# Softplus attention: softplus as one activation function, its square divided among three engines, experts picked by rank, loops written out

## The chip, the cores and the metric

The kernel runs on one core of a Trainium2 chip. A core has five engines that work through queues of their own and meet at semaphores: TensorE (PE in the profile, its weight loads PEld), VectorE (DVE), ScalarE (ACT), GpSimd (POOL) and SyncE (SP, which issues DMA transfers here). The metric is the device time of one execution in microseconds, lower is better.

## The reference, cut to what matters

The program is a chain of six stages on `x` of shape (4, 1024, 256): a gated recurrent feed-forward, an attention, the feed-forward again, a mixture of experts, a state-space layer, the mixture again. The change touches the attention's inner function and the choice of experts:

```
scores = einsum('bhqd,bhkd->bhqk', q, k) * hs ** (-0.5)      # 16 heads of 16, t = 1024
p = softplus(scores);  p = p * p;  p = p * causal
attn = p / (sum(p, -1) + 1e-09)
out = einsum('bhqk,bhkd->bhqd', attn, v)

gates = softmax(x @ gate_w.T + gate_b)                       # 8 experts
top_gates, top_idx = top_k(gates, 2)
expert_out = einsum('bsh,eoh->bseo', x, expert_w) + expert_b
result = (take(expert_out, top_idx) * top_gates).sum(2)
```

## The kernel before

The stages follow one another, each in a `Phase` that ends with a barrier of all engines: load, feed-forward (`ffn_phase`), queries, keys and values (`qkv_phase`), attention (`attention_phase`), projection, feed-forward, mixture (`moe_phase`), state space (`ssm_phase`), mixture. Each engine's program is written by hand; the order in it is the order of the code, and counted semaphores join the engines. Most stages write their first and last round out and put the rounds between into a hardware loop (`Fori`), in which places and counts come from registers.

**Attention.** Four heads are one pass over 1024 queries; 16 passes make the stage, two to a body, so eight bodies, of which the first and the last are written out and six come from a loop. A pass is cut into 18 units (`pass_units`), a body into `NU` = 36. The queries come in two blocks of 512. Units 0 to 3 are the first block's tiles on the causal diagonal ("rest" units: two pieces per head, each with a small matmul with `neg` that masks it), unit 4 holds its upper pieces in one half-wide bank; units 5 to 12 are the second block's full tiles of 512 columns, 13 to 16 its rest units, 17 its upper unit. So a pass has 8 full, 8 rest and 2 upper units; the first two kinds are 128x1024 numbers, an upper one 128x512.

A unit passes through these hands:

- PE, `score_unit` (L1346, mask L1349, upper unit's mask L1338): scores into one of three pairs of PSUM banks (`SU` = 3).
- ACT, `exp` (L1408): exp of the scores into the weights tile `Wt` in SBUF, which holds `WU` = 12 units; then `ln` (L1414): ln(1 + that), in place. Together they are softplus.
- DVE, `softplus` (L1445): the larger of that and the score itself, which guards large scores; it reads the scores' bank a last time, in two instructions, and so frees it for PE (`max_done`).
- POOL (L1508): the square, in place (`sq_pool`).
- PE, `value_unit` (L1369): the squares times the values and a column of ones, in fp32, into one of two output banks, one for each query block.

PE's program puts the scores of unit u + 7 (`AHEAD`) ahead of the value products of unit u. A block that is complete is copied out by DVE (L1452, 7 units after the block's end), turned by PE (`turn_output`, L1378, 4 units after it), and on DVE the row sums are inverted (L1458, L1460, 9 units after) and the output divided (L1467, 10 units after), which sets `o_done`. PE waits for `o_done` before the first value products of the same query block in the next pass. For the second query block, whose last unit is 17, that is unit 23, while its turn stands behind the value products of unit 21. POOL also copies the values of a pass into `v_ones` (L1499, L1501).

**Mixture.** 16 groups of 512 rows in each of two stages run on PE in matmuls of 512 columns (L48); DVE adds each expert's result, scaled by its gate, to `X` (L932), from a ring of four PSUM banks. In the middle of a group's last tile DVE chooses the experts of the next group (`choose`): softmax, the eight largest by `max` (L899), their places (L902), the first two places compared with a row of numbers `iota` (L908), both added (L912), times half the gates (L914), then a split for PE (L917, L919).

## Time and profile before

| what | us |
|---|---|
| median of 3 runs (1795.97 to 1798.01) | 1797.84 |
| the profiled execution, span from first to last instruction | 1794.8 |
| PE busy in the span | 1683.5 (94%) |
| DVE busy | 1295.7 (72%) |
| ACT busy | 1092.9 (61%) |
| POOL busy | 858.2 (48%) |
| attention, PE's first to last instruction | 274.5 to 815.1 |

The profiled execution's own span is 3.0 us below the median of the runs, which also hold what lies around the span. The profile is read by stage, since each stage is limited by something else. Matmuls are pipelined and the ends of their records are modelled, so a PE that counts as busy may still be waiting; the distance between the starts of two matmuls tells more than a record's length.

### The profile page before, as it was taken

How to read it: one execution, taken by the hardware profiler on the slowest of the kernel's cores; microseconds unless marked ns; L12 is line 12 of the kernel's file. 1: busy time of each engine (PE TensorE's matmuls, PEld its weight loads, DVE VectorE, ACT ScalarE, POOL GpSimd, SP SyncE). 2: the span in 40 equal slices, each digit the busy share in tenths (PEclk: the TensorE clock that was granted, in tenths of full speed). 3: DMA queues.
4: the chain of work that ended last, by engine and by line, in shares of the span. 5: the costliest groups of instructions: out<-in, count | busy, mean ns of one | idle time of the engine just before them, and what ended most of it. 6: DMA issues, size and time to landing. Idle time of an engine off the chain costs nothing. (4 is left out here: it accounts for less than half of the span.)

```text
span 1794.8 us, 33269 instructions
## 1 busy us (share of the span) xinstructions
PE 1683.5 (94%) x11188; PEld 1158.1 (65%) x11188; DVE 1295.7 (72%) x2830; ACT 1092.9 (61%) x1612; POOL 858.2 (48%) x654
## 2 busy tenths in 40 slices
PE   8999897999999999998999899998899999889999
PEld 7888773333333333338788777777677777667777
DVE  5455885777777777775545788886787787778886
ACT  3332788999999999993333322214888887722120
POOL 0002108999999999995003322211265665411111
PEclk9999998999999999999999999999999999999999
DMA  5000275635535535400000100001232233200000
GB/s 164 1 0 12 91 214 90 76 48 73 68 47 73 67 47 79 62 1 1 13 1 30 29 7 0 0 0 39 83 96 95 104 112 103 95 1 24 23 23 24
DMA packets 57112, 95.09 MB, mean 53 GB/s; under 512 B 7904, under 2 KB 29632, under 8 KB 57024
## 3 DMA queue, kind: packets, MB, share of 16 engines
q1 hardware_dynamic: 56064, 93.35, 24.0%
q8 instruction: 51, 0.84, 0.2%
q10 hardware_dynamic: 960, 0.59, 0.1%
q14 instruction: 37, 0.30, 0.1%
HBM read 76.88 MB, written 17.04 MB: 52 GB/s over the span
## 5 line engine op out<-in xcount | busy, mean ns | idle before, releaser
L1508 POOL TENSOR_TENSOR att_weights<-att_weights 128x1024 f32<-128x1024 f32 (+1 forms) x288 | 508.9, 1799 | 9.0 <-DVE att_weights L1445 5.6
L1445 DVE SCALAR_TENSOR_TENSOR att_weights<-att_weights,ps 128x512 f32<-128x512 f32 x544 | 348.2, 684 | 145.1 <-ACT att_weights L1414 138.6
L932 DVE SCALAR_TENSOR_TENSOR X<-ps,moe_gsel,X 128x256 f32 (+1 forms) x512 | 246.6, 484 | 63.1 <-PE ps L48 44.8
L1369 PE MATMUL ps<-att_weights,att_v_ones 64*32 64x64 f32 (+5 forms) x2048 | 289.0, 399 | 1.9 <-POOL att_weights L1508 1.8
L1414 ACT ACTIVATE att_weights<-att_weights 128x1024 f32<-128x1024 f32 (+1 forms) x288 | 286.5, 1007 | 1.0
L1408 ACT ACTIVATE att_weights<-ps 128x1024 f32<-128x1024 f32 (+1 forms) x288 | 278.4, 972 | 8.6 <-PE ps L1349 7.0
L48 PE MATMUL ps<-w_experts_hi,moe_xh 128*128 128x512 f32 x512 | 205.3, 401 | 0.4 <-DVE X L932 0.4
L48 PE MATMUL ps<-w_experts_hi,moe_xl 128*128 128x512 f32 x512 | 203.2, 397 | 0.0
L48 PE MATMUL ps<-w_experts_lo,moe_xh 128*128 128x512 f32 x512 | 201.6, 394 | 0.0
L1369 PEld LDWEIGHTS ps<-att_weights,att_v_ones 128*32 128x32 f32 (+1 forms) x2048 | 82.4, 108 | 104.6 <-issue 80.2
L424 ACT ACTIVATE ffn_gates<-ps,ffn_gate_bias 128x512 f32<-128x512 f32 x72 | 49.5, 688 | 147.5 <-PE ps L48 143.2
L998 POOL TENSOR_TENSOR X<-X,moe_bias_sb 128x512 f32 (+1 forms) x32 | 41.3, 1290 | 193.6 <-DVE X L932 170.8
L1346 PE MATMUL ps<-q_stack,k_stack 128*64 128x64 bf16 (+5 forms) x640 | 103.8, 274 | 23.3 <-DVE att_weights L1445 14.9
L104 POOL TENSOR_TENSOR ffn_rstd<-ffn_var,ffn_power 128x4 f32<-128x4 f32 x14 | 14.1, 1008 | 219.6 <-DVE ffn_var L136 219.6
L1346 PE MATMUL ps<-att_q_stack,att_k_stack 128*64 128x64 bf16 (+5 forms) x640 | 100.5, 267 | 17.0 <-DVE att_weights L1445 13.0
L48 PEld LDWEIGHTS ps<-w_experts_hi,moe_xh 128*128 128x128 f32 x512 | 96.1, 188 | 27.5 <-DVE X L932 4.0
L2172 POOL TENSOR_TENSOR ssm_rise<-ssm_rise,ssm_cT 128x512 f32<-128x512 f32 x56 | 87.8, 1588 | 48.4 <-DVE ssm_xc L2035 37.0
L48 PEld LDWEIGHTS ps<-w_experts_lo,moe_xh 128*128 128x128 f32 x512 | 96.1, 188 | 22.3
L1346 PEld LDWEIGHTS ps<-q_stack,k_stack 128*128 128x128 bf16 (+1 forms) x640 | 42.0, 105 | 104.7 <-DVE att_weights L1445 74.9
L48 PEld LDWEIGHTS ps<-w_experts_hi,moe_xl 128*128 128x128 f32 x512 | 96.2, 188 | 20.4
L1346 PEld LDWEIGHTS ps<-att_q_stack,att_k_stack 128*128 128x128 bf16 (+1 forms) x640 | 40.8, 103 | 98.1 <-DVE att_weights L1445 72.2
L833 ACT ACTIVATE moe_gT<-ps 96x512 fp32r<-96x512 f32 x16 | 9.5, 595 | 155.1 <-PE ps L764 155.1
(282 smaller groups left out, 3796.3 us busy)
## 6 DMA issues: line engine op xcount, KB each, us to landing
ssm_lb<-decays SPq DMA_DIRECT2D x32, 512.0 KB, 4.7
ssm_rise<-decays SPq DMA_DIRECT2D x28, 512.0 KB, 3.9
qk_parts<-qkv_part SPq DMA_DIRECT2D x32, 384.0 KB, 2.7
q_stack<-qk_parts SPq DMA_DIRECT2D x64, 128.0 KB, 4.9
k_stack<-qk_parts SPq DMA_DIRECT2D x64, 128.0 KB, 8.4
att_q_stack<-qk_parts SPq DMA_DIRECT2D x64, 128.0 KB, 4.7
att_k_stack<-qk_parts SPq DMA_DIRECT2D x64, 128.0 KB, 8.5
out<-X SPq DMA_DIRECT2D x7, 512.0 KB, 2.9
```

The costliest lines, as they stand in the source:

```text
L48: ins = pe.matmul(out, l(k), r(k), start=first and n == 0, stop=last and n == len(passes) - 1)
L104: pool.tensor_tensor(self.rstd[:, s], self.var[:, s], self.power[:, :], ALU.pow).then_inc(self.rstd_done, 1)
L424: act.activation(gates[:, m, gate], ring[:, u % RING], ACT.Tanh if gate == 2 else ACT.Sigmoid, bias=bias[:, gate * KC + m:gate * KC + m + ...
L932: dve.scalar_tensor_tensor(out=x, in0=ring[:, e // 2, (e % 2) * C:(e % 2 + 1) * C], scalar=gsel[:, s, j, e:e + 1], in1=x, op0=ALU.mult, op ...
L998: pool.tensor_tensor(x, x, bias_sb[:, turn], ALU.add).then_inc(added, 1)
L1346: ins = pe.matmul(scores(u)[rows, t, c:c + w], SK[s][:, h, keys], SQ[s][:, h, q:q + w], start=not upper, stop=n >= len(segments) - 2 if up ...
L1369: ins = pe.matmul(O(qb)[h * 2 * HD:(h + 1) * 2 * HD, q0:q0 + w], values, Wt[rows, u % WU, t, c:c + w], start=kj == 0 and part == FULL, sto ...
L1408: act.activation(Wt[:, u % WU, 0:n], scores(u)[:, 0:n], ACT.Exp).then_inc(exp_done, 1)
L1414: act.activation(wt, wt, ACT.Ln, bias=1.0).then_inc(ln_done, 1)
L1445: dve.scalar_tensor_tensor(out=wt[:, t], in0=wt[:, t], scalar=LIMIT, in1=scores(u)[:, t], op0=ALU.min, op1=ALU.max).then_inc(max_done, 2 // n)
L1508: pool.tensor_tensor(wt, wt, wt, ALU.mult).then_inc(sq_pool, 1)
L2172: ins = pool.tensor_tensor(heads, heads, cT[:, v, b].unsqueeze(1).broadcast_to([P, NH // 2, P]), ALU.mult)
```

## The change

1. Attention: ACT applies `Softplus` once, straight from the scores' bank (L1405 of the changed kernel), in place of exp and ln; DVE's step with the maximum is gone. `p_done`, set by ACT, frees the bank for PE, in one wait per unit where there were two. The square is divided: of the 18 units of a pass ACT squares units 8 and 14 (L1410), POOL unit 11 (L1495), DVE the other 15 (L1432), 13 of them 128x1024 and two 128x512. PE waits for the engine that squared the unit.
2. Mixture: instead of maxima and places, DVE compares all pairs of the 8 gates (128x256 numbers for four tiles), equal and greater; equal counts only against an earlier expert (`earlier`, a table of 8x8), the two are added and summed to a rank, and gates of rank under 2 are kept.
3. Every `Fori` becomes a Python loop, so all rounds are written out with constant places and counts.

```diff
@@ -895,23 +894,20 @@
                                   ALU.mult).then_inc(prob_done, 1)
                 dve.wait_ge(prob_done, n + 1)
                 dve.tensor_scalar(half[:, :, :], prob[:, :, :], 0.5, None, ALU.mult)
-                for j in range(GT):
-                    dve.max(best[:, j], prob[:, j])
-                dve.drain()
-                for j in range(GT):
-                    ins = dve.max_index(place[:, j], best[:, j], prob[:, j])
-                ins.then_inc(place_done, 1)
-                dve.wait_ge(place_done, n + 1)
-                dve.tensor_copy(placef[:, :, :], place[:, :, 0:2]).then_inc(placef_done, 1)
-                dve.wait_ge(placef_done, n + 1)
-                for r in range(2):
-                    ins = dve.tensor_tensor(pick[:, r], iota[:, :].unsqueeze(1).broadcast_to([P, GT, E]),
-                                            placef[:, :, r:r + 1].broadcast_to([P, GT, E]), ALU.is_equal)
-                ins.then_inc(pick_done, 1)
-                dve.wait_ge(pick_done, n + 1)
-                dve.tensor_tensor(pick[:, 0], pick[:, 0], pick[:, 1], ALU.add).then_inc(both_done, 1)
-                dve.wait_ge(both_done, n + 1)
-                dve.tensor_tensor(gsel[:, s], half[:, :, :], pick[:, 0], ALU.mult).then_inc(gsel_done, 1)
+                others = prob[:, :, :].unsqueeze(2).broadcast_to([P, GT, E, E])
+                own = prob[:, :, :].unsqueeze(3).broadcast_to([P, GT, E, E])
+                dve.tensor_tensor(level[:, :, :, :], others, own, ALU.is_equal).then_inc(level_done, 1)
+                dve.tensor_tensor(above[:, :, :, :], others, own, ALU.is_gt)
+                dve.wait_ge(level_done, n + 1)
+                dve.tensor_tensor(level[:, :, :, :], level[:, :, :, :], earlier[:, :, :].unsqueeze(1).broadcast_to([P, GT, E, E]),
+                                  ALU.mult).then_inc(earlier_done, 1)
+                dve.wait_ge(earlier_done, n + 1)
+                dve.tensor_tensor(above[:, :, :, :], above[:, :, :, :], level[:, :, :, :], ALU.add).then_inc(above_done, 1)
+                dve.wait_ge(above_done, n + 1)
+                dve.tensor_reduce(rank[:, :, :], above[:, :, :, :], AX.X, ALU.add).then_inc(rank_done, 1)
+                dve.wait_ge(rank_done, n + 1)
+                dve.scalar_tensor_tensor(out=gsel[:, s], in0=rank[:, :, :], scalar=2.0, in1=half[:, :, :],
+                                         op0=ALU.is_lt, op1=ALU.mult).then_inc(gsel_done, 1)
                 dve.wait_ge(gsel_done, n + 1)
                 dve.wait_ge(gT_turned, n)
                 dve.tensor_copy(g3[:, :, 0:TERMS:2, 0:E], gsel[:, s].unsqueeze(2).broadcast_to([P, GT, 2, E])).then_inc(g3_hi, 1)
...
@@ -1285,7 +1281,12 @@
     TURN_LAG, COPY_LAG, DEN_LAG, OUT_LAG = 4, 7, 9, 10
     SU, WU = 3, 12
     assert NU % SU == 0 and NU % WU == 0
-    LIMIT = 60.0
+    BY_ACT, BY_POOL = (8, 14), (11,)
+    squarer = ["act" if u % PU in BY_ACT else "pool" if u % PU in BY_POOL else "dve" for u in range(NU)]
+
+    def squares(by, i, u):
+
+        return i * squarer.count(by) + squarer[:u + 1].count(by)
 
     def outputs_at(x, ends, n, lag, i, first, stage):
 
...
@@ -1328,19 +1329,15 @@
                 s, segments = u // PU, pass_units[u % PU]
                 if u % PU == 0:
                     pe.wait_ge(loaded[s], (i + 1) * (16 * 2 * COPIES))
-                half = -1
                 upper = segments[0][-1] == UPPER
+                pe.wait_ge(p_done, i * NU + u + 1)
                 if upper:
                     low = slice(0, HALF)
-                    pe.wait_ge(max_done, 2 * (i * NU + u) + 1)
                     pe.sem_inc(scores_free, 1)
                     for r in range(2):
                         pe.matmul(scores(u)[r * HALF:(r + 1) * HALF, 0].rearrange("p (s q) -> p s q", q=HALF), neg[low, low],
                                   ident16[low, low].unsqueeze(1).broadcast_to([HALF, BANK // HALF, HALF]), start=True, stop=False)
                 for n, (h, kj, t, c, q, w, part) in enumerate(segments):
-                    if t != half and not upper:
-                        half = t
-                        pe.wait_ge(max_done, 2 * (i * NU + u) + t + 1)
                     rows = slice(h % 2 * HALF, (h % 2 + 1) * HALF) if part == UPPER else slice(0, P)
                     keys = slice(kj * P, kj * P + (HALF if part == UPPER else P))
                     ins = pe.matmul(scores(u)[rows, t, c:c + w], SK[s][:, h, keys], SQ[s][:, h, q:q + w],
@@ -1358,7 +1355,7 @@
                     pe.wait_ge(o_done, (i * 2 + s) * BLOCKS + qb + 1)
                     if qb == 0:
                         pe.matmul(O(qb), ident16[:, :], neg[:, 0:1].broadcast_to([P, BANK]), start=True, stop=False)
-                pe.wait_ge(sq_pool, i * NU + u + 1)
+                pe.wait_ge(sq_done[squarer[u]], squares(squarer[u], i, u))
                 if products[0][-1] == UPPER:
                     pe.sem_inc(squared, 1)
                 for h, kj, unit, t, c, q, w, part in products:
@@ -1390,60 +1387,49 @@
             for u in range(AHEAD):
                 score_unit(0, u)
             body(0, first=True)
-            with pe.Fori(1, BODIES - 1) as i:
+            for i in range(1, BODIES - 1):
                 body(i)
             body(BODIES - 1, last=True)
 
         @block.scalar
         def _(act):
-            act.preload_act_table_set(LN_EXP_SET)
-
-            def exp(i, u):
+            act.preload_act_table_set(SOFTPLUS_SET)
+
+            def softplus(i, u):
                 i, u = i + u // NU, u % NU
                 act.wait_ge(s_done, i * NU + u + 1)
 
                 before = step_of[u - WU] + NS if u >= WU else step_of[u - WU + NU]
                 act.wait_ge(pv_done, i * NS + before + 1)
                 n = BANKS[u % PU]
-                act.activation(Wt[:, u % WU, 0:n], scores(u)[:, 0:n], ACT.Exp).then_inc(exp_done, 1)
-
-            def ln(i, u):
-                i, u = i + u // NU, u % NU
-                act.wait_ge(exp_done, i * NU + u + 1)
+                act.activation(Wt[:, u % WU, 0:n], scores(u)[:, 0:n], ACT.Softplus).then_inc(p_done, 1)
+
+            def square(i, u):
+                act.wait_ge(p_done, SU + i * NU + u + 1)
                 wt = Wt[:, u % WU, 0:BANKS[u % PU]]
-                act.activation(wt, wt, ACT.Ln, bias=1.0).then_inc(ln_done, 1)
-
-            def body(i, first=False, last=False):
+                act.activation(wt, wt, ACT.Square).then_inc(sq_done["act"], 1)
+
+            def body(i, last=False):
                 for u in range(NU):
-                    narrow, behind = BANKS[u % PU] == 1, BANKS[u % PU - 1] == 1 and not (first and u == 0)
-                    if narrow:
-                        ln(i, u)
                     if not (last and u == NU - 1):
-                        exp(i, u + 1)
-                        if narrow:
-                            ln(i, u + 1)
-                    if not narrow and not behind:
-                        ln(i, u)
+                        softplus(i, u + 1)
+                    if squarer[u] == "act":
+                        square(i, u)
 
             act.sem_inc(o_turned, 2)
             act.sem_inc(o_done, 2)
             act.sem_inc(pv_done, NS)
-            exp(0, 0)
-            body(0, first=True)
-            with act.Fori(1, BODIES - 1) as i:
-                body(i)
-            body(BODIES - 1, last=True)
+            act.sem_inc(p_done, SU)
+            softplus(0, 0)
+            for i in range(BODIES):
+                body(i, last=i == BODIES - 1)
 
         @block.vector
         def _(dve):
-            def softplus(i, u):
-
-                wt = Wt[:, u % WU]
-                dve.wait_ge(ln_done, i * NU + u + 1)
-                n = BANKS[u % PU]
-                for t in range(n):
-                    dve.scalar_tensor_tensor(out=wt[:, t], in0=wt[:, t], scalar=LIMIT, in1=scores(u)[:, t],
-                                             op0=ALU.min, op1=ALU.max).then_inc(max_done, 2 // n)
+            def square(i, u):
+                dve.wait_ge(p_done, SU + i * NU + u + 1)
+                wt = Wt[:, u % WU, 0:BANKS[u % PU]]
+                dve.tensor_tensor(wt, wt, wt, ALU.mult).then_inc(sq_done["dve"], 1)
 
             def copy_output(n, i, k):
 
@@ -1469,7 +1455,8 @@
 
             def body(i, first=False, last=False):
                 for u in range(NU):
-                    softplus(i, u)
+                    if squarer[u] == "dve":
+                        square(i, u)
                     outputs_at(u, BLOCK_UNITS, NU, COPY_LAG, i, first, copy_output)
                     outputs_at(u, BLOCK_UNITS, NU, DEN_LAG, i, first, invert_sums)
                     outputs_at(u, BLOCK_UNITS, NU, OUT_LAG, i, first, divide_output)
@@ -1478,9 +1465,8 @@
                     outputs_left(BLOCK_UNITS, NU, DEN_LAG, i, invert_sums)
                     outputs_left(BLOCK_UNITS, NU, OUT_LAG, i, divide_output)
 
-            dve.sem_inc(max_done, 2 * SU)
             body(0, first=True)
-            with dve.Fori(1, BODIES - 1) as i:
+            for i in range(1, BODIES - 1):
                 body(i)
             body(BODIES - 1, last=True)
 
@@ -1503,23 +1489,24 @@
 
             def body(i, last=False):
                 for u in range(NU):
-                    pool.wait_ge(max_done, 2 * (SU + i * NU + u + 1))
-                    wt = Wt[:, u % WU, 0:BANKS[u % PU]]
-                    pool.tensor_tensor(wt, wt, wt, ALU.mult).then_inc(sq_pool, 1)
+                    if squarer[u] == "pool":
+                        pool.wait_ge(p_done, SU + i * NU + u + 1)
+                        wt = Wt[:, u % WU, 0:BANKS[u % PU]]
+                        pool.tensor_tensor(wt, wt, wt, ALU.mult).then_inc(sq_done["pool"], 1)
                     if u == NU // 3:
                         copy_v(i, 1, (i + 1) * NS)
                     if u == NU * 5 // 6 and not last:
                         copy_v(i + 1, 0, (i + 1) * NS + PS)
 
             copy_v(0, 0, 0)
-            with pool.Fori(0, BODIES - 1) as i:
+            for i in range(0, BODIES - 1):
                 body(i)
             body(BODIES - 1, last=True)
 
         @block.sync
         def _(sp):
             load_stacks(sp, stacks, loaded, parts_dram, 0, 1, STACKED)
-            with sp.Fori(1, BODIES) as i:
+            for i in range(1, BODIES):
                 for s in range(2):
                     sp.wait_ge(s_done, i * NU + (s - 1) * (NU // 2))
                     load_stacks(sp, stacks, loaded, parts_dram, i, s, STACKED)
```

The loops of the other stages change like the attention's, and `iota` gives way to `earlier` where the mixture is called.

ACT's queue in the attention, where `att_weights` is the tile `Wt` and `ps` the scores. Before, from the stage's start, exp (L1408) and ln (L1414):

```order
L1399 ACT_TABLE_LOAD
L1408 ACTIVATE att_weights<-ps 128x1024 x2
L1414 ACTIVATE att_weights<-att_weights 128x1024
L1408 ACTIVATE att_weights<-ps 128x1024
L1414 ACTIVATE att_weights<-att_weights 128x1024
L1408 ACTIVATE att_weights<-ps 128x1024
L1414 ACTIVATE att_weights<-att_weights 128x1024
L1408 ACTIVATE att_weights<-ps 128x512
```

Now the first pass, softplus (L1405) and ACT's own squares (L1410):

```order
L1405 ACTIVATE att_weights<-ps 128x1024 x4
L1405 ACTIVATE att_weights<-ps 128x512
L1405 ACTIVATE att_weights<-ps 128x1024 x5
L1410 ACTIVATE att_weights<-att_weights 128x1024
L1405 ACTIVATE att_weights<-ps 128x1024 x6
L1410 ACTIVATE att_weights<-att_weights 128x1024
L1405 ACTIVATE att_weights<-ps 128x1024
```

Two instructions to a unit became one, and two to a pass came in.

DVE's queue in the attention where a query block's output is finished, in the first body. Before:

```order
L1452 COPY att_oT<-ps 128x512
L1445 SCALAR_TENSOR_TENSOR att_weights<-att_weights,ps 128x512 x4
L1458 TENSOR_SCALAR att_den<-ps 128x16
L1460 RECIPROCAL att_den<-att_den 128x16
L1445 SCALAR_TENSOR_TENSOR att_weights<-att_weights,ps 128x512 x2
L1467 TENSOR_TENSOR v<-ps,att_den 128x256
```

Now, for the second query block:

```order
L1438 COPY att_oT<-ps 128x512
L1432 TENSOR_TENSOR att_weights<-att_weights 128x1024
L1444 TENSOR_SCALAR att_den<-ps 128x16
L1446 RECIPROCAL att_den<-att_den 128x16
L1432 TENSOR_TENSOR att_weights<-att_weights 128x1024
L1453 TENSOR_TENSOR v<-ps,att_den 128x256
```

The pair of half-wide maxima between the inversion and the division gave way to one square.

## Rows read from the trace of the kernel before

**Rows 1.** Busy time by engine, attention (length, PE, PEld, DVE, ACT, POOL, PEclk, DMA share).

```profile
274.00:816.00 542.00, 497.78 (x4560) 196.38 (x4560) 390.93 (x672) 524.78 (x577) 526.85 (x322) 0.99 0.44 59
```

**Rows 2.** Timeline, POOL, one pass (start, length, engine, line, operation, count).

```profile
504.48 0.61 POOL L1499 COPY att_v_ones<-v 128x512 f32 x1
...
505.82 32.03 POOL L1508 TENSOR_TENSOR att_weights<-att_weights 128x1024 f32<-128x1024 f32 x18 [0.17 <-DVE att_weights L1445]
```

**Rows 3.** Groups by line and shape, ACT (busy, mean ns of one, idle before).

```profile
L1414 ACT ACTIVATE att_weights<-att_weights 128x1024 f32<-128x1024 f32 x256 | 269.9, 1054 | 1.0
L1408 ACT ACTIVATE att_weights<-ps 128x1024 f32<-128x1024 f32 x256 | 259.5, 1020 | 8.6 <-PE ps L1349 7.0 <-PE ps L1346 0.4
...
L1962 ACT ACTIVATE ssm_xc<-ssm_xc 128x1024 f32<-128x1024 f32 x16 | 16.2, 1061 | 0.2 <-DVE ssm_xc L2035 0.2
```

**Rows 4.** Timeline, PE, stretches of the attention without a wait.

```profile
519.48 0.24 PE L1369 MATMUL ps<-att_weights,att_v_ones 64*32 64x64 f32 x1
...
520.06 0.61 PE L1346 MATMUL ps<-att_q_stack,att_k_stack 128*128 128x512 bf16 x2
...
520.81 1.06 PE L1369 MATMUL ps<-att_weights,att_v_ones 128*32 128x448 f32 x8
521.80 0.60 PE L1346 MATMUL ps<-att_q_stack,att_k_stack 128*128 128x512 bf16 x2
522.33 1.06 PE L1369 MATMUL ps<-att_weights,att_v_ones 128*32 128x448 f32 x8
...
539.42 0.40 PE L1338 MATMUL ps<-ident,neg 64*64 64x512 bf16 x2
...
540.13 1.05 PE L1369 MATMUL ps<-att_weights,att_v_ones 128*32 128x512 f32 x4
...
543.34 0.36 PE L1346 MATMUL ps<-q_stack,k_stack 128*128 128x448 bf16 x1
...
543.99 1.05 PE L1369 MATMUL ps<-att_weights,att_v_ones 128*32 128x512 f32 x4
544.98 0.31 PE L1346 MATMUL ps<-q_stack,k_stack 128*128 128x320 bf16 x1
```

**Rows 5.** Groups by line and shape, DVE: products and sums of two SBUF operands.

```profile
L294 DVE TENSOR_TENSOR v<-v,ffn_hc 128x1024 f32<-128x1024 f32 x8 | 9.7, 1219 | 2.0 <-DVEq L1193 2.0
...
L457 DVE TENSOR_TENSOR ffn_gates<-ffn_gates 128x512 f32<-128x512 f32 x24 | 17.5, 730 | 41.5 <-ACT ffn_gates L424 41.5
```

**Rows 6.** Timeline, PE and DVE, from a turn to the division.

```profile
503.99 0.66 PE L1378 MATMUL ps<-ident,att_oT 128*128 128x128 f32 x4
...
504.48 0.30 PE L1346 MATMUL ps<-q_stack,k_stack 128*128 128x320 bf16 x1
...
504.68 0.17 DVE L1458 TENSOR_SCALAR att_den<-ps 128x16 f32<-128x16 f32 x1 [0.18 <-PE ps L1378]
...
505.11 1.28 DVE L1445 SCALAR_TENSOR_TENSOR att_weights<-att_weights,ps 128x512 f32<-128x512 f32 x2
...
506.31 0.42 DVE L1467 TENSOR_TENSOR v<-ps,att_den 128x256 f32 x1
```

**Rows 7.** Busy time by engine, start of the attention (columns as in rows 1).

```profile
274.00:286.00 12.00, 7.93 (x54) 3.71 (x54) 5.46 (x9) 11.07 (x12) 9.18 (x7) 0.50 0.93 133
```

**Rows 8.** Timeline, DVE, one choice of experts in the first mixture.

```profile
1128.24 0.37 DVE L899 MAX8 moe_best<-moe_prob 128x8 f32<-128x8 f32 x4
...
1130.34 0.20 DVE L917 CAST moe_g<-moe_gsel 128x64 fp32r<-128x64 f32 x1
```

**Rows 9.** Waits, first mixture, 1045 to 1205 us (six groups).

```profile
PEld ps L48 <- DVE X L932: 1.6, 6, 0.3
```

**Rows 10.** Timeline, DVE, the first choice of the first mixture.

```profile
1026.10 1.05 DVE L905 CAST moe_placef<-moe_place 128x8 f32<-128x8 uint32 x1
```

**Rows 11.** DMA queues (packets, MB, share): instructions 290 to 430 us; all 430 to 750 us.

```profile
q8 instruction: 9, 0.15, 0.6%
...
q1 hardware_dynamic: 12311, 20.20, 47.3%
```

59 lines of the change are left out of this document (29 added, 30 removed).

## The prediction

> **What bounds the kernel now.** I read busy time by stretch first. In the attention, 542 us of the span, ACT is busy 524.8 us and POOL 526.9 [rows 1]. Then the timeline: POOL runs 18 squares in 32.0 us without a gap, and with its copies (1.34 us from the first copy to the first square) a pass takes 33.3 us [rows 2]; 16 passes are 533 of the 540.6 us between PE's first and last instruction. ACT needs as long: ln and exp cost 1.054 and 1.020 us a unit [rows 3], overlap a little at their edges, and leave it full as well. So the attention is bound by ACT and POOL together, and PE's 497.8 us of records [rows 1] must not be taken for work, since their ends are modelled. What PE needs by itself is read from distances between starts, in stretches where nothing was waited for [rows 4]:
>
> - scores of a full unit 522.33 - 521.80 = 0.53 us, of a rest unit 543.99 - 543.34 = 0.65, of an upper unit 540.13 - 539.42 = 0.71;
> - value products of a full unit 544.98 - 543.99 = 0.99, of a rest unit 521.80 - 520.81 = 0.99, of an upper unit 520.06 - 519.48 = 0.58;
> - one turn 504.48 - 503.99 = 0.49 [rows 6]; the filling of one output bank, once a pass, (520.81 - 520.06) - 0.53 = 0.22 [rows 4].
>
> A pass has 8 full, 8 rest and 2 upper units and two turns: 8 x 0.53 + 8 x 0.65 + 2 x 0.71 + 16 x 0.99 + 2 x 0.58 + 2 x 0.49 + 0.22 = 29.1 us. PE could do a pass in 29.1 us and gets one per 33.3.
>
> **Attention, who does what after the change.** ACT keeps 16 wide and 2 narrow functions, which I price like exp, and adds two squares priced like ln, the same shape in place: 16 x 1.02 + 2 x 0.6 (a little over half) + 2 x 1.05 = 19.6 us a pass. Softplus has no row. Three other forms of the same width stand at 1.020, 1.054 and 1.061 us [rows 3], so one application should cost about 1.02; the upper bound is that of the two it replaces, 2.07. DVE loses the maxima (1.28 us a unit, two instructions [rows 6]) and gets 13 wide and 2 narrow products of two SBUF operands at 1.22 and 0.73 [rows 5], 17.3 us, beside an estimated 3 us for two output blocks (copy, sums, inversion, division, by the lengths in rows 6): 20.4. POOL keeps one square and the copies, about 3.2. All of them are under 29.1, so **PE becomes the bound**, and the stage costs 16 x 29.1 = 466 us plus what PE still waits for.
>
> The wait that I see coming is for the output bank. The turn of a pass's second block stands behind value unit 21, the bank is filled again at value unit 23. After the turn's start DVE needs 0.69 us to begin the sums, 1.12 to reach the next square, and the division ended 506.73 - 503.99 = 2.74 us after it [rows 6]; a wide square lasts as long as the two maxima did, so this stays. PE gets back to that bank in 0.49 (turn) + 0.53 (scores of unit 29) + 0.58 (value unit 22, upper) + 0.53 (scores of unit 30) = 2.1 us. That leaves 0.6 us, 15 times: 9 us. Before, PE came later and this was covered.
>
> The score banks don't stall PE: between the end of a unit's scores and the scores three units on lie three value products and two more score units, over 4 us, and ACT needs at most a square and a softplus, 2.1. Squares have seven units of lead, some 11 us. At the start three score units go at once and four more at ACT's pace, and PEclk was 0.50 from 274 to 286 us [rows 7], which cost nothing while PE waited and now does; I put 5 us (between 2, if the clock returns soon, and 8, if all of that stretch runs at half speed). The end, one block out after the last product, is 2 us. Attention: 466 + 9 + 5 + 2 = 482, so **58.6 us less**.
>
> **Mixture.** Between the first maximum and the split DVE spends 1130.34 - 1128.24 = 2.10 us [rows 8]. The new chain has five operations over 256 numbers, for which the division of 128x256 at 0.42 [rows 6] is the nearest row, and a small one: 5 x 0.42 + 0.19 + steps between dependent ones of about 0.04 - 0.09 where the two comparisons overlap = 2.35. PE already waits 1.6 us for DVE in six groups [rows 9], so its ring is just used up there and the 0.25 passes through: 14 x 0.25 = 3.5. Bounds are -0.1 and +0.6 a group, -1 and +8. In the first choice POOL is still splitting weights, and a cast of only 128x8 took 1.05 us there [rows 10]; the five longer operations can lose more there, so I add 1.5 (0 to 5). Together +5.
>
> A rule bears on that place. The Trainium skill, "SBUF — State Buffer" (section "Who interferes with whom"), says that a VectorE instruction with two SBUF inputs and a GpSimd instruction that reads SBUF exclude each other for the whole instruction. That speaks against this change, since DVE's new squares read SBUF twice where the maxima read PSUM once; it is the second rival below.
>
> **Loops.** Nothing is taken off the path. Between 430 and 750 us, where five rounds of the loop run, only the data queue moved anything [rows 11], so a round that is repeated loads no code, and every pass there took the same 33.3 us as elsewhere. Written out, code must be loaded all the time: in 290 to 430 us nine pieces came, 0.6% of 16 engines over 140 us, 1.5 us each [rows 11], for about two bodies, beside work that did not slow. At the new pace a body lasts about 59 us and asks for 4.5 pieces, one in 13 us, so this is hidden: I put -1 for the registers and branches saved.
>
> The Trainium skill, "Runtime: NRT & Kernel Launch" (section "Instruction fetch mechanics"), says that a branch to a place outside the loaded window waits for its code to be fetched, and advises writing loops out. This trace doesn't agree, by the missing instruction queue in rows 11. By the rule PE's 14 taken branches at 1.5 us would give another 21 us, an estimate that the sum does without.
>
> **Sum.** 1794.8 - 58.6 + 5 - 1 = 1740 for the profiled span. That execution's span stands 3.0 us below the median of 1797.84, so the median becomes **1743 us**, 3.0% less.
>
> **Rivals.**
>
> 1. *Softplus costs as much as the two functions together*, and ACT stays the bound. ACT's pass is then today's 33.3 us with two squares more, 35.4, and the attention grows by 16 x 2.1 = 34 us: 1797.8 + 34 + 4 = **1836 us**, slower. It decides from the point where 16 wide and 2 narrow functions and 2.1 us of squares exceed 29.7 (about 1.6 us for a wide one); slower than before only from about 1.8. For it: no row shows this function. Against: forms of one width lie within 4% of each other [rows 3]. 5%.
> 2. *DVE and POOL block each other where it hurts*: POOL's square of unit 29 (1.8 us) falls between the inversion and the division, and PE's wait for the bank grows from 0.6 to 2.4 us, 15 times 1.8: **1770 us**. Against: unit 29's softplus ends only about 2.3 us after the turn's start, when DVE's square has begun; elsewhere DVE has 8 us to spare in a pass. 7%.
> 3. *Code comes too late.* About 4.5 pieces a body in eight bodies at 1.5 us are 54 us, all of the gain if none is hidden: **1797 us**, no change. Against: the written-out rounds in 290 to 430 us kept their pace. With half of it, 1770, which the range holds. 5%.
> 4. *The change doesn't remove the bound*, because PE's own pass is longer than 29.1: if the waits of PE were caused by PE, the attention would stay at 33.3. Against it are the stretches of rows 4, the same matmuls at both paces. 2%, no change.
>
> **Numbers.** PE as the bound at about 29.7 us a pass has 81%. Its terms reach from 1728 (no wait for the bank, start at 2, mixture at 0, a little more from the registers) to 1758 (start at 8, mixture at 13, one more microsecond in half of the passes). The range goes on to 1770 to take in the second rival and half of the third: 1728 to 1770. A measurement here can tell 0.2%, 3.6 us, from no change. Of rival 3's 5 points I give 2 to a gain that survives in part, 2 to no change and 1 to a loss. So faster by more than that is 81 + 7 + 2 = 90%, within it 2 + 2 (rival 4) = 4%, slower 5 + 1 = 6%.
>
> **What would show it.** Right: ACT's softplus near 1.02 us and DVE's squares near 1.22; PE's distances as in rows 4 and about 0.6 us of wait for the division before value unit 23; ACT, DVE and POOL idle between units; attention near 482 us; the choice from the comparisons to the split near 2.35 us. Wrong: softplus above 1.6 us; PE waiting for squares in units other than 23; waits of PE on nothing the profile shows, in step with instruction pieces; a choice longer than 2.7 us.

## The result and the profile after

The changed kernel takes **1729.2 us** (median of 4 runs, 1725.55 to 1729.62) where the kernel before takes 1797.09 (4 runs): ratio 0.9615, 95% interval 0.9603 to 0.9628. Forecast was 1743 us, in a range from 1728 to 1770. Faster was right, and so was PE as the new bound; the gain is 68 us and not 55, so the time came out near the lower end of the range. The profiled execution's span is 1727.8 us (before 1794.8).

The span and the busy time of each engine from the page of the changed kernel, and its busy time in the attention (length, PE, PEld, DVE, ACT, POOL, PEclk, DMA share, GB/s), which answers to [rows 1]:

```profile
span 1727.8 us, 28806 instructions
...
PE 1643.6 (95%) x11141; PEld 1148.6 (66%) x11188; DVE 1244.1 (72%) x2350; ACT 878.2 (51%) x1356; POOL 412.0 (24%) x382
...
274.00:749.00 475.00, 457.86 (x4513) 186.23 (x4560) 337.38 (x368) 310.64 (x321) 80.76 (x50) 0.99 0.49 68
```

The attention's own instructions now cover 473.7 us where they covered 541.7. The other stages together moved by 1.0 us. ACT and POOL, full before, are at 65% and 17% there, DVE at 71%. PE is the bound: in all but the last pass, which has no scores behind it, the second turn stands 29.57 us behind that of the pass before, where 33.3 us stood before the change. Two neighbours, 553.47 - 523.90 = 29.57 (start, length, engine, line, what, count):

```profile
523.90 0.66 PE L1375 MATMUL ps<-ident,att_oT 128*128 128x128 f32 x4
...
553.47 0.66 PE L1375 MATMUL ps<-ident,att_oT 128*128 128x128 f32 x4
```

The costliest groups of the attention (busy, mean ns of one, idle before and what ended it); they answer to [rows 2, 3, 5]:

```profile
L1405 ACT ACTIVATE att_weights<-ps 128x1024 f32<-128x1024 f32 (+1 forms) x288 | 280.7, 976 | 157.1 <-PE ps L1346 83.0
L1432 DVE TENSOR_TENSOR att_weights<-att_weights 128x1024 f32<-128x1024 f32 (+1 forms) x240 | 298.5, 1262 | 67.8 <-ACT att_weights L1405 67.1
L1366 PE MATMUL ps<-att_weights,att_v_ones 64*32 64x64 f32 (+5 forms) x2048 | 286.8, 398 | 6.2 <-DVE v L1453 6.2
...
L1495 POOL TENSOR_TENSOR att_weights<-att_weights 128x1024 f32<-128x1024 f32 x16 | 30.3, 1892 | 378.0 <-ACT att_weights L1405 378.0
```

Read the idle columns: ACT, DVE and POOL all wait for the scores or the softplus, while PE's value products waited 6.2 us in all, for the division. (PE's scores have 11.8 us of idle time: 4.3 at the stage's start, and 7.5 on nothing that the profile shows, 0.16 us at a time, where one of the two records of a full unit's scores is missing from the trace.) The softplus costs 0.976 us on average over 256 wide and 32 narrow ones, where exp cost 0.972; a wide one alone costs 1.023, where exp cost 1.020 [rows 3]. That disposes of the first rival.

The wait for the output bank is where it was expected. PE's timeline at the end of a pass (start, length, engine, line, what, count, idle before):

```profile
525.73 0.38 PE L1343 MATMUL ps<-q_stack,k_stack 128*128 128x512 bf16 x1 [0.16 <-issue]
526.52 1.05 PE L1366 MATMUL ps<-att_weights,att_v_ones 128*32 128x512 f32 x4 [0.41 <-DVE v L1453]
```

526.52 - 525.73 = 0.79 us, where value products follow the second half of a full unit's scores after 0.31 us at 95 other places of the stage; 0.48 us of wait, 15 times: 7.2 us.

DVE and POOL around that point show a lock of which the second rival spoke:

```profile
524.80 0.25 DVE L1446 RECIPROCAL att_den<-att_den 128x16 f32<-128x16 f32 x1
524.97 1.16 DVE L1432 TENSOR_TENSOR att_weights<-att_weights 128x1024 f32<-128x1024 f32 x1
526.05 0.41 DVE L1453 TENSOR_TENSOR v<-ps,att_den 128x256 f32<-128x256 f32 x1
526.38 2.79 DVE L1432 TENSOR_TENSOR att_weights<-att_weights 128x1024 f32<-128x1024 f32 x1
...
526.20 1.89 POOL L1495 TENSOR_TENSOR att_weights<-att_weights 128x1024 f32<-128x1024 f32 x1 [24.60 <-ACT att_weights L1405]
```

DVE's second square lasts 2.79 us in place of 1.16: it ends 1.08 us behind the end of POOL's square (526.20 + 1.89 = 528.09), as if it had begun then. It stands behind the division, where DVE has time to spare, so the lock costs nothing here. Whether it would cost something elsewhere is experiment 4.

### The profile page after: what moved, and what is told of

Its sections match the earlier page's. It is cut to its first block and busy times, and to the rows that moved or that the text cites. A ratio compares the mean times of both kernels' runs of the same rounds, so it can differ in the third digit from the quotient of the medians.

```text
span 1727.8 us, 28806 instructions
## 1 busy us (share of the span) xinstructions
PE 1643.6 (95%) x11141; PEld 1148.6 (66%) x11188; DVE 1244.1 (72%) x2350; ACT 878.2 (51%) x1356; POOL 412.0 (24%) x382
## 5 line engine op out<-in xcount | busy, mean ns | idle before, releaser
L1405 ACT ACTIVATE att_weights<-ps 128x1024 f32<-128x1024 f32 (+1 forms) x288 | 280.7, 976 | 157.1 <-PE ps L1346 83.0
L1432 DVE TENSOR_TENSOR att_weights<-att_weights 128x1024 f32<-128x1024 f32 (+1 forms) x240 | 298.5, 1262 | 67.8 <-ACT att_weights L1405 67.1
L928 DVE SCALAR_TENSOR_TENSOR X<-ps,moe_gsel,X 128x256 f32<-128x256 f32 x512 | 246.1, 483 | 63.5 <-PE ps L48 40.4
L1495 POOL TENSOR_TENSOR att_weights<-att_weights 128x1024 f32<-128x1024 f32 x16 | 30.3, 1892 | 378.0 <-ACT att_weights L1405 378.0
L1343 PE MATMUL ps<-q_stack,k_stack 128*64 128x64 bf16 (+5 forms) x617 | 86.5, 266 | 8.0 <-ACTq L1421 4.3
L1343 PE MATMUL ps<-att_q_stack,att_k_stack 128*64 128x64 bf16 (+5 forms) x616 | 84.9, 262 | 3.8 <-issue 3.8
L994 POOL TENSOR_TENSOR X<-X,moe_bias_sb 128x512 f32<-128x512 f32 x32 | 41.3, 1291 | 193.8 <-DVE X L928 171.9
L1343 PEld LDWEIGHTS ps<-q_stack,k_stack 128*128 128x128 bf16 (+1 forms) x640 | 37.8, 105 | 66.4 <-issue 46.1
L1916 ACT ACTIVATE ssm_dec<-ssm_lb,ssm_l_tok 128x128 f32<-128x128 f32 x248 | 75.6, 388 | 8.2 <-PE ps L1796 6.6
L1343 PEld LDWEIGHTS ps<-att_q_stack,att_k_stack 128*128 128x128 bf16 (+1 forms) x640 | 36.9, 103 | 63.3 <-issue 42.0
L2022 DVE SCALAR_TENSOR_TENSOR ssm_xc<-ssm_xpad,ssm_conv_w,ssm_xc 128x512 f32<-128x512 f32 x96 | 77.0, 810 | 2.3
```

The lines of the kernel that those rows point to most:

```text
L928: dve.scalar_tensor_tensor(out=x, in0=ring[:, e // 2, (e % 2) * C:(e % 2 + 1) * C], scalar=gsel[:, s, j, e:e + 1], in1=x, op0=ALU.mult, op ...
L994: pool.tensor_tensor(x, x, bias_sb[:, turn], ALU.add).then_inc(added, 1)
L1343: ins = pe.matmul(scores(u)[rows, t, c:c + w], SK[s][:, h, keys], SQ[s][:, h, q:q + w], start=not upper, stop=n >= len(segments) - 2 if up ...
L1405: act.activation(Wt[:, u % WU, 0:n], scores(u)[:, 0:n], ACT.Softplus).then_inc(p_done, 1)
L1432: dve.tensor_tensor(wt, wt, wt, ALU.mult).then_inc(sq_done["dve"], 1)
L1495: pool.tensor_tensor(wt, wt, wt, ALU.mult).then_inc(sq_done["pool"], 1)
```

## The experiments

Eleven kernels were run, each beside the kernel before on its chip; ratios and intervals are to that kernel. The questions: is PE the bound and the bank's wait a real one (1), what does each part of the change do alone (5 to 8), would the lock have hurt (4), and why does PE's tail at the end of the stage run faster than its rows said (2, 3, 9 to 11). That tail is the last eight value units, seven wide ones and an upper one: scores run seven units ahead, so those of the last unit (L1338 and `128*64` below) stand ahead of the eighth value unit from the end, and none come behind:

```profile
741.88 0.44 PE L1343 MATMUL ps<-att_q_stack,att_k_stack 128*64 128x64 bf16 x16
742.25 3.81 PE L1366 MATMUL ps<-att_weights,att_v_ones 128*32 128x512 f32 x45
745.82 0.24 PE L1366 MATMUL ps<-att_weights,att_v_ones_up 64*32 64x64 f32 x1
```

Seven wide units take 745.82 - 742.25 = 3.57 us, 0.51 each, where [rows 4] had 0.99: about half. The expectation of experiment 2 reads them as 0.90 apart and takes the 0.09 us for a cost of each change between scores and values; experiment 3 builds on that. It is a misreading, and the runs fell outside both.

**1. The division directly behind the inversion.**

```diff
-    TURN_LAG, COPY_LAG, DEN_LAG, OUT_LAG = 4, 7, 9, 10
+    TURN_LAG, COPY_LAG, DEN_LAG, OUT_LAG = 4, 7, 9, 9
```

> The changed kernel with the division of an output block directly behind the inversion of its row sums, ahead of DVE's next square (OUT_LAG 9 in place of 10). Theory (PE is the bound, and the only wait left in a pass is the one for the output bank, 0.48 us at 15 places): that wait goes, the pass falls from 29.57 to 29.1 us and the time by about 7 us, to about 1722 us. Rival (the 0.48 us is PE's own, an artefact of where the trace puts a wait, or it comes back as a wait for the square that is now later): 1729 us, same as the changed kernel.

1721.5 us, ratio 0.9579 (0.9563 to 0.9595); the group of value products has no idle time left. A pass takes 29.09 us. The wait was real and is gone, 7 to 8 us less than the changed kernel, and nothing took its place.

```profile
L1366 PE MATMUL ps<-att_weights,att_v_ones 64*32 64x64 f32 (+5 forms) x2048 | 286.8, 398 | 0.0
```

**2. Two score units, then two value units.**

```diff
-                    if not (last and u + AHEAD >= NU):
-                        score_unit(i, u + AHEAD)
+                    for ahead in (u + AHEAD, u + AHEAD + 1) if u % 2 == 0 else ():
+                        if not (last and ahead >= NU):
+                            score_unit(i, ahead)
                     value_unit(i, u)
```

> The changed kernel with PE's program in pairs: two score units, then two value units, in place of one and one. The work is the same; the changes between score matmuls (weights of 128 by 128) and value matmuls (four strips of 32 columns) are halved. Theory (about 0.09 us of each value unit's 0.99 belongs to that change, since the last seven value units of the stage, with no scores between them, stand 0.90 apart): 288 changes fewer at about 0.09 us, 26 us less, about 1703 us. Rival (the 0.09 us at the stage's end has another cause, such as scores that no longer compete for anything): within 3 us of the changed kernel, 1729 us; and if score banks now run short, since two score units stand back to back, slower than that, with PE waiting for the softplus.

1630.44 us, ratio 0.9078 (0.9063 to 0.9093). That is 99 us less than the changed kernel, four times what the theory gave and outside both expectations. The theory fell. PE's timeline shows what happens: first two value units side by side, then one that a turn parts from its neighbour.

```profile
520.73 0.19 PE L1346 MATMUL ps<-ident,neg 128*128 128x64 bf16 x1
520.85 1.07 PE L1366 MATMUL ps<-att_weights,att_v_ones 128*32 128x512 f32 x8
521.85 0.31 PE L1343 MATMUL ps<-q_stack,k_stack 128*128 128x320 bf16 x1
...
523.06 1.05 PE L1366 MATMUL ps<-att_weights,att_v_ones 128*32 128x512 f32 x4
524.04 0.66 PE L1375 MATMUL ps<-ident,att_oT 128*128 128x128 f32 x4
```

Eight records, two units, take 521.85 - 520.85 = 1.00 us; four records, one unit, take 524.04 - 523.06 = 0.98. A unit holds two of a pass's four heads, and each head's value products have weights of 32 columns and write 32 rows of the output bank. So one unit uses half of PE's width, and two neighbouring units that hold different heads run at the same time, if no matmul over the full width stands between them. The Trainium skill, "TensorE: Matmul & The Clock Gate" (section "Part 3: Packing small matmuls — row/col tiling"), says that matmuls whose outputs lie in different groups of 32 partitions run at the same time; this trace agrees, 1.00 us for two units in place of 1.96.

**3. Both.**

> Both edits together: score and value units in pairs, and the division directly behind the inversion. If the two effects are separate costs on PE's own path they add up: by the theory about 1729 - 26 - 7 = 1696 us. If they share a slack (the pairs move PE's return to the output bank, so that the wait grows or goes by itself), the gain is that of the larger one, about 1703 us.

1622.35 us, ratio 0.9029 (0.9014 to 0.9044): 8 us less than the pairs alone, as experiment 1 had. The two effects add up.

**4. POOL's square one unit earlier.**

```diff
-    BY_ACT, BY_POOL = (8, 14), (11,)
+    BY_ACT, BY_POOL = (8, 14), (10,)
```

> The changed kernel with POOL's square on unit 10 of a pass in place of unit 11 (and DVE's on 11 in place of 10), so that POOL's square of about 1.9 us falls nearer to the inversion and the division of the second block. It tests the second rival of the prediction, that DVE and POOL exclude each other there. If they exclude each other for whole instructions, the division comes up to 1.1 us later at 15 places, and the time is up to 16 us longer, about 1745 us. If they run beside each other: within 2 us of the changed kernel, 1729 us, with DVE's inversion and division as long as they were.

1751.71 us, ratio 0.9744 (0.9728 to 0.976): 22.5 us slower than the changed kernel, where the expectation gave the lock up to 16. DVE, POOL and PE, at the end of a pass:

```profile
535.10 1.89 POOL L1495 TENSOR_TENSOR att_weights<-att_weights 128x1024 f32<-128x1024 f32 x1 [26.15 <-ACT att_weights L1405]
...
535.38 0.25 DVE L1446 RECIPROCAL att_den<-att_den 128x16 f32<-128x16 f32 x1
535.55 2.52 DVE L1432 TENSOR_TENSOR att_weights<-att_weights 128x1024 f32<-128x1024 f32 x1
538.00 0.41 DVE L1453 TENSOR_TENSOR v<-ps,att_den 128x256 f32<-128x256 f32 x1
...
538.46 1.05 PE L1366 MATMUL ps<-att_weights,att_v_ones 128*32 128x512 f32 x4 [1.77 <-DVE v L1453]
```

The square between inversion and division lasts 2.52 us in place of 1.16, and PE's wait grows from 0.41 to 1.77: 1.36 us, 15 times, 20 us. In two of the fifteen passes the granted clock also fell behind this wait, and the pass took 32.5 us in place of 30.94, 3 us for both. One of the two (columns as in [rows 1], PEclk 1.00 and then 0.57):

```profile
440.00:444.00 4.00, 2.14 (x41) 1.19 (x40) 3.18 (x5) 2.62 (x3) 3.29 (x2) 1.00 0.00 0
444.00:448.00 4.00, 3.92 (x16) 0.98 (x16) 3.02 (x5) 1.02 (x1) 1.43 (x2) 0.57 0.00 0
```

The short instructions on either side are as long as they were, the inversion (0.25) beside POOL's square too. The Trainium skill, "SBUF — State Buffer" (section "Who interferes with whom"), which the prediction cited, is borne out: the product of two SBUF operands is shut out for the whole of POOL's instruction. The second rival is a true mechanism, kept out of the changed kernel by one unit.

**5. The kernel before with its loops written out.** Every `with eng.Fori(a, b) as i:` of the kernel before becomes `for i in range(a, b):`.

> The kernel before with its loops written out and nothing else changed. The prediction's term: -1 us for registers and branches, 1796 us. Its third rival (code comes too late when all rounds are written out): PE or ACT wait in step with instruction pieces, up to some 50 us more, 1850 us; by half of it 1820. The rule of the Trainium skill that a branch waits for its code: a gain of some 20 us, 1777 us.

1792.75 us (9 runs), ratio 0.9974 (0.9964 to 0.9984): 4.6 us less (2.9 to 6.5). No late code, and no 20 us either. The attention gave 2.0 us of it. In the mixture the distance between two choices, 26.02 to 26.19 us in turn before, is 26.04 to 26.05 from the second choice of each stage on. The first maxima of three choices in turn:

```profile
1073.99 0.37 DVE L899 MAX8 moe_best<-moe_prob 128x8 f32<-128x8 f32 x4
...
1100.04 0.36 DVE L899 MAX8 moe_best<-moe_prob 128x8 f32<-128x8 f32 x4
...
1126.08 0.36 DVE L899 MAX8 moe_best<-moe_prob 128x8 f32<-128x8 f32 x4
```

**6. The same with the choice by rank.** To experiment 5 comes the changed kernel's `choose`.

> The kernel before with its loops written out and the choice of experts by rank, the attention unchanged; against the run with the loops alone this is the mixture's term by itself. The prediction had +5 us (3.5 for 14 choices that come 0.25 us later, 1.5 for the first ones). The trace of the changed kernel gives the two mixture stages together only 0.6 us more. If the ring of four PSUM banks covers the later choice: 0 to 1 us more than the loops alone. If it passes through: 5 us more.

1794.24 us (9 runs), ratio 0.9981 (0.997 to 0.9991), 1.3 us more than with the loops alone by the ratios (1.5 by the medians), which is less than the two intervals can tell from nothing. The trace tells more: the distance between choices is 26.08 to 26.09 in place of 26.05, 0.035 us a group, apart from single longer ones (26.43 once); in the first mixture the distance from the first choice to the second is 25.01 in place of 24.75, in the second mixture it stays (23.57 and 23.58). The first comparisons of three choices in turn:

```profile
1076.55 0.42 DVE L899 TENSOR_TENSOR moe_level<-moe_prob 128x256 f32<-128x256 f32 x1
...
1102.64 0.42 DVE L899 TENSOR_TENSOR moe_level<-moe_prob 128x256 f32<-128x256 f32 x1
...
1128.72 0.42 DVE L899 TENSOR_TENSOR moe_level<-moe_prob 128x256 f32<-128x256 f32 x1
```

**7. All squares on POOL.**

```diff
-    BY_ACT, BY_POOL = (8, 14), (11,)
+    BY_ACT, BY_POOL = (), tuple(range(PU))
```

> The changed kernel with all squares left on POOL: softplus as one function and no maximum, but nothing divided. Theory (before, ACT and POOL were both full, so neither half of the change is worth much alone): POOL's 18 squares at 1.78 us and its copies set the pass, 33.3 us as before, so 1729 + 16 x 3.7 = 1789 us. Rival (POOL was slowed by DVE's maxima, which read the same SBUF tile, and now runs freely): squares near 1.6 us, pass near 30 us, about 1740 us.

1782.76 us, ratio 0.9916 (0.99 to 0.9933). A pass on POOL:

```profile
433.28 0.61 POOL L1485 COPY att_v_ones<-v 128x512 f32<-128x512 f32 x1
433.95 0.40 POOL L1487 COPY att_v_ones_up<-v 64x256 f32<-64x256 f32 x1
434.42 31.65 POOL L1495 TENSOR_TENSOR att_weights<-att_weights 128x1024 f32<-128x1024 f32 x18
466.01 0.61 POOL L1485 COPY att_v_ones<-v 128x512 f32<-128x512 f32 x1
```

466.01 - 433.28 = 32.7 us a pass; a wide square stays at 1.89 us without DVE's maxima beside it, so the rival of this expectation falls. Saving a function on ACT, and DVE's maximum, is worth 15 us of the 68 while POOL keeps the squares, and some 3 of these 15 belong to the loops and the choice (experiment 6).

**8. Two passes of ACT over each unit.** ACT copies each unit in place after the softplus, and the squares wait for that; the copy is not needed and changes no value.

```diff
+            def again(i, u):
+                act.wait_ge(p_done, SU + i * NU + u + 1)
+                wt = Wt[:, u % WU, 0:BANKS[u % PU]]
+                act.activation(wt, wt, ACT.Copy).then_inc(again_done, 1)
...
+                    again(i, u)
```

> The changed kernel with a second pass of ACT over every unit (a copy in place between softplus and square, which leaves the values as they are): the division of the squares without the saving of a function, and the first rival's price for softplus. The second function is priced like ln, 1.054 us wide. Theory: ACT is the bound at 16 x (0.98 to 1.02 + 1.054) + 2 x 1.2 + 2 x 1.05 = 37 us at most, 35.4 by the first rival's working, a pass: 1729 + 16 x 5.8 = 1822 us, up to 1845, so dividing the squares alone makes the kernel slower than before. Rival (ACT has room, because the trace of before showed it full only by its waits for POOL): under 1800 us.

1827.52 us, ratio 1.0169 (1.0152 to 1.0186).

```profile
L1405 ACT ACTIVATE att_weights<-ps 128x1024 f32<-128x1024 f32 (+1 forms) x288 | 286.0, 993 | 21.0 <-PE ps L1346 21.0
L1410 ACT ACTIVATE att_weights<-att_weights 128x1024 f32<-128x1024 f32 (+1 forms) x288 | 297.0, 1032 | 0.0
```

ACT is full again and the kernel is slower than before, within 9 us of the first rival's 1836. Part of this is PE's: its mean granted clock in the attention is 0.93 here (0.99 before), and the 21 us that ACT waits are for PE's scores. So neither half alone brings the gain: dividing the squares in this way without the single function loses 30 us, the single function without the division gains 15, both together gain 68.

**9. The pairs with half of them on the same heads.** To tell the overlap of strips from a saving on changes of kind, two units were exchanged in every second tile of experiment 2's kernel:

```diff
-        for together in tiles:
-            at = len(pass_units)
-            for pair in range(2):
+        for step, together in enumerate(tiles):
+            at, odd = len(pass_units), step % 2
+            for pair in (odd, 1 - odd):
...
-            pass_steps.append((qb, at + 1, [(h, kj, at + h // 2, h % 2, c, q, w, part)
+            pass_steps.append((qb, at + 1, [(h, kj, at + (h // 2 ^ odd), h % 2, c, q, w, part)
```

> The kernel in pairs, with the two units of every second tile exchanged, so that heads 2 and 3 come before heads 0 and 1 there. The work and the number of changes between score and value matmuls are those of the kernel in pairs; but the two value units of four more pairs of a pass (units 6 and 7, 10 and 11, 12 and 13, 14 and 15) now hold the same two heads, so they write the same two strips of 32 columns and not all four. Theory formed on the trace of the kernel in pairs (a value unit uses two of PE's four strips, and two units on different strips run at the same time, 1.0 us for both in place of 0.98 each): four overlaps of about 0.95 us less in 16 passes, 61 us more than the kernel in pairs, about 1690 us. Rival (the gain comes from fewer changes between the two kinds of matmul): the same as the kernel in pairs, 1630 us.

1682.79 us, ratio 0.9364 (0.9348 to 0.9379): 52 us slower than the pairs, with the same work and the same number of changes.

```profile
482.12 1.91 PE L1366 MATMUL ps<-att_weights,att_v_ones 128*32 128x512 f32 x8
483.96 0.36 PE L1343 MATMUL ps<-q_stack,k_stack 128*128 128x448 bf16 x1
...
493.95 1.08 PE L1366 MATMUL ps<-att_weights,att_v_ones 128*32 128x448 f32 x16
494.97 1.04 PE L1343 MATMUL ps<-q_stack,k_stack 128*128 128x512 bf16 x4
```

Two units on the same heads take 483.96 - 482.12 = 1.84 us for their eight records; two units on different heads, further on, 494.97 - 493.95 = 1.02 us for sixteen. The strips are the cause; a price on changes of kind is excluded as the main one. Units on the same strips also add into the same 32 rows of the output bank, and these runs don't tell the strip from the rows. The expectation put 0.95 us on each lost overlap; by the rows it is 1.84 - 1.00 = 0.84, and 4 x 0.84 in 16 passes are 54 us, near the 52 measured.

**10. The turn out of the pair.** To experiment 3:

```diff
-                    outputs_at(u, BLOCK_UNITS, NU, TURN_LAG, i, first, turn_output)
+                    for back in (u - 1, u) if u % 2 else ():
+                        outputs_at(back, BLOCK_UNITS, NU, TURN_LAG, i, first, turn_output)
```

> Pairs and division directly behind the inversion, and the turn of the first block's outputs moved from between value units 8 and 9 of a pass to behind unit 9, so that it no longer parts a pair. By the theory of the strips one more overlap of about 0.95 us in 16 passes: 15 us less than the 1622 us of pairs with the early division, about 1607 us. DVE is busy 91% there, so it may become the bound: 1612 us at worst by DVE's 20.9 us of a 22.9 us pass leaving some 2 us a pass. By the rival (fewer changes of kind), a turn behind unit 9 saves at most one change: 1617 us.

1606.37 us, ratio 0.894 (0.8925 to 0.8955); a pass takes 21.69 us where experiment 3's takes 22.66, so the turn behind the pair gives one more overlap, as the theory of the strips had it.

**11. And POOL's square to ACT.** `BY_ACT, BY_POOL = (8, 11, 14), ()`.

> As the last kernel, with POOL's square (unit 11) given to ACT, so that ACT squares 3 units of a pass and POOL none. DVE's square beside POOL's lasts 2.8 us in place of 1.2, so DVE gains 1.6 us a pass, and ACT has 1.05 us more (about 20 us of a pass of 22). If DVE is a bound by now: faster than the last kernel, by up to 10 us. If PE is still the bound: within 3 us of it. If ACT is late with the next softplus: slower.

1606.03 us, ratio 0.894 (0.8925 to 0.8955), the same. Busy time in the middle of the attention, experiment 10 and then 11 (columns as in [rows 1]):

```profile
400.00:500.00 100.00, 100.00 (x1324) 48.57 (x1325) 95.83 (x109) 84.47 (x93) 21.60 (x14) 1.00 0.66 100
```

```profile
400.00:500.00 100.00, 100.00 (x1321) 48.42 (x1317) 87.75 (x107) 87.15 (x97) 16.77 (x10) 1.00 0.71 102
```

DVE falls from 96% to 88% and the time stays, so PE is still the bound there. Both beat the kernel before by 10.6% and the changed kernel by 123 us.

## What the prediction had right, and which of its terms failed

The path was right: PE becomes the bound, at the price of a pass that was predicted. What failed is the sizing of the other terms of the sum, nearly all too high. Above all, "the 0.25 passes through" in the mixture failed: +5 us were put there, and the runs showed about +1. Next come the price of 0.99 us for a value unit wherever it stands, which the stage's tail undercut by 3.4 us in all, and the start, put at 5 us and measured at 2.1. The points below take them one by one.

- **PE becomes the bound, a pass 29.1 us plus the bank's wait.** Right: 29.57 - 0.48 = 29.09 by the trace, and experiment 1 took the wait away alone. The wait was put at 0.6 us, 9 us in all; it is 0.48, 7.2 in all: 1.8 us too much.
- **ACT, DVE and POOL fall below PE.** Right, with most of the prices taken: a wide square on DVE has a median of 1.224 us (1.22 predicted; the mean is 1.351, with those that wait for POOL), ACT's square a mean of 1.048 (1.05), POOL's 1.892, and a wide softplus 1.023 (1.02). POOL's copies were not foreseen: a mean of 1.60 and 1.44 us in place of 0.61 and 0.40, so POOL has 4.9 us a pass and not 3.2, which costs nothing here. Experiments 7 and 8 show that both halves are needed for it.
- **"At the start ... I put 5 us"** failed by 2.9. From the first scores to the first value products pass 282.74 - 275.56 = 7.18 us. The scores of eight units (the seven that run ahead, and the next one) and the filling of the bank stand there, 4 x 0.65 + 0.71 + 3 x 0.53 + 0.22 = 5.12 us at the prices of the prediction: the start costs 2.1.

```profile
275.56 0.53 PE L1343 MATMUL ps<-q_stack,k_stack 128*128 128x448 bf16 x1 [4.25 <-ACTq L1421]
...
282.43 0.38 PE L1357 MATMUL ps<-neg,ident 128*128 128x512 bf16 x1
282.74 1.06 PE L1366 MATMUL ps<-att_weights,att_v_ones 128*32 128x448 f32 x8
```

  PEclk in the first stretches of the attention, to be read beside [rows 7], where it stayed at 0.50:

```profile
278.00:281.00 3.00, 3.00 (x34) 1.98 (x32) 3.00 (x3) 2.91 (x3) 2.79 (x3) 0.50 1.03 139
281.00:284.00 3.00, 2.77 (x22) 1.10 (x17) 3.00 (x4) 2.88 (x5) 0.00 (x0) 0.96 1.05 139
```

  The full clock, 2.4 GHz, came back at about 281, with PE at work almost without a gap from 275.56 on; before, PE was stopped by waits here and PEclk stayed at 0.50, 1.2 GHz, up to 288. The lower bound of 2 assumed a clock that returns soon, and was the value.
- **"The end ... is 2 us"** failed, and with it the reading under it: 0.99 us was taken as what a value unit costs PE, wherever it stands. It is what a unit costs between scores. The last eight were in the sum with 7 x 0.99 + 0.58 = 7.5 us and took 745.82 - 742.25 + 0.58 = 4.15. This is worth only 3.4 us in the changed kernel, but the same reading hid the 99 us of experiment 2: 29.1 us was the floor of this order of PE's program, not of its work. No rival spoke of it, and the rows could not show it, since [rows 4] has value units between scores alone.
- **"Mixture: together +5"** failed. The choice itself grew less than thought, from 2.10 [rows 8] to 1062.82 - 1060.56 = 2.26 us (2.35 predicted):

```profile
1060.56 0.42 DVE L899 TENSOR_TENSOR moe_level<-moe_prob 128x256 f32<-128x256 f32 x1
...
1062.82 0.20 DVE L913 CAST moe_g<-moe_gsel 128x64 fp32r<-128x64 f32 x1
```

  And it doesn't pass through. Of the 0.16 us, 0.035 reach the distance between choices (26.05 to 26.085, experiments 5 and 6), 14 x 0.035 = 0.5 us; the first choice of the first mixture (0.26) and a few longer distances add most of the rest of the 1.3 us of experiment 6. The first choice had been given 1.5. PE's small wait in [rows 9] was no sign of a ring just used up: in the first mixture PE's weight loads waited 2.3 us for DVE before and 2.3 after.
- **"Loops: -1"** was too small a gain by itself, -4.6 (-2.9 to -6.5) in experiment 5. But 2.0 of it lay in the attention, on engines that no longer bind. The third rival, code too late, shows in no pass of the changed kernel: between 300 and 748 us 43 pieces of code came, and the distance between turns stayed at 29.57. The estimate of 21 us, which the prediction made of the rule of the Trainium skill, "Runtime: NRT & Kernel Launch" (section "Instruction fetch mechanics"), is not borne out by these 4.6 us; whether the loops' branches leave the loaded window, on which the rule depends, no run shows.

In sum, the attention shrank by 68.0 us where 58.6 were forecast: 9.4 more, of which the bank is 1.8, the start 2.9, the tail 3.4, the way out behind the last product 0.5 (747.94 - 746.4 = 1.5 us in place of 2), and 0.6 the rounding of 16 x 29.09 = 465.4 to 466; that leaves 0.2 us. The other stages, mixture and loops together, were forecast at +5 - 1 = +4 and moved by +1.0, of which the two mixture stages are 0.6: 3.0 less. 9.4 + 3.0 is the distance of the span from the forecast, 1740 - 1727.8 = 12.2, but for rounding. Nearly every error had one sign: the start (2 to 8) and the mixture (-1 to 13 with its first choice) were put near the middle of wide bounds and came out near the lower ends, 2.1 and about 1. The main term was exact.

The ends of the range don't follow from the terms that the prediction names for them. Without the wait for the bank (9), with the start at 2 and the mixture at 0, 1743 us become 1726, and less with the registers, not 1728; with the start at 8, the mixture at 13 and 8 us more in the passes they become 1762, not 1758. The measured 1729.2 lies inside either way, but with the wait for the bank still there: it is the other terms that were too high.

## What to carry to other kernels

When an engine becomes the bound, ask whether its floor is that of the work or that of the order: look for one place in the trace where the same instructions run without their neighbours (here the stage's tail, 0.51 us a unit in place of 0.99). Matmuls with few output columns should stand beside others that use the remaining strips, with no full-width matmul between them. Small costs on both sides of the main term should be taken at the value of the nearest row that has the same conditions, not in the middle of wide bounds, since several of them can add up with one sign.

## What the runs showed of the hardware that was not expected

- Value products of 32 output columns use half of PE as they are ordered here: two units take 1.00 us together on different strips (experiment 2), 1.84 us on the same ones (experiment 9), and one alone 0.98, each from the start of its first record to the start of the next instruction.
- A product of two SBUF operands on DVE waits out POOL's whole square: 2.52 to 2.79 us in place of 1.16, while an inversion of 128x16 beside it stays at 0.25 (experiment 4), and a division that reads PSUM and SBUF at 0.41 (the changed kernel, and experiment 4 beside POOL's copy).
- POOL's copies of the values, 0.61 and 0.40 us when DVE makes no squares (experiment 7), last 1.61 and 1.28 us beside DVE's squares (experiment 4; 1.60 and 1.44 on average in the changed kernel).
- A loop's round cost some 0.2 us in the mixture: two groups make a round, and two distances between choices are 26.11 + 26.18 = 52.29 us with the loop and 2 x 26.05 = 52.10 without (experiment 5).
- A wait of PE of 1.77 us was followed by a fall of the granted clock in two passes of experiment 4 (0.57 over 4 us) and by none in the other thirteen.
